# A cross-attention with 16 heads of 16: two passes after one another, or side by side

## The reference

```python
def _L0_xattn_ref(q, k, v, Wq, bq, Wk, bk, Wv, bv, Wo, bo, mask):
    H = 16
    NEG = -10000000000.0
    B, S, D = q.shape
    dk = D // H
    qh = (q @ Wq.T + bq).reshape(B, S, H, dk).transpose(0, 2, 1, 3)
    kh = (k @ Wk.T + bk).reshape(B, S, H, dk).transpose(0, 2, 1, 3)
    vh = (v @ Wv.T + bv).reshape(B, S, H, dk).transpose(0, 2, 1, 3)
    scores = jnp.einsum('bhqd,bhkd->bhqk', qh, kh) / jnp.sqrt(jnp.float32(dk))
    scores = jnp.where(mask[:, None, :, :] == 0, jnp.float32(NEG), scores)
    attn = jax.nn.softmax(scores, axis=-1)
    ctx = jnp.einsum('bhqk,bhkd->bhqd', attn, vh)
    concat = ctx.transpose(0, 2, 1, 3).reshape(B, S, D)
    return concat @ Wo.T + bo
...
    x = x + _L0_xattn_ref(_layernorm(x, axis=-1), ctx_1024, ctx_1024, L0_xattn_Wq, ...
```

## Time and profile before

| | us |
|---|---|
| timed runs | 2060.04, 2058.66, 2054.0 |
| median | 2058.66 |
| profiled execution | 2057.15 |
| its span | 2055.3 |
| mean granted clock of TensorE | 0.878 of full speed |

### The profile page before, as it was taken

How to read it: one execution, slowest core, us unless ns; L and a number is a source line. 1 busy time by engine, 2 the same in 40 slices (tenths; PEclk the granted TensorE clock), 3 DMA queues, 4 the chain that set the end, 5 groups by cost and what they waited for, 6 DMA issues and landing times. The chain is left out here.

```text
span 2055.3 us, 32700 instructions
## 1 busy us (share of the span) xinstructions
PE 1573.8 (77%) x11346; PEld 1345.9 (65%) x11346; DVE 876.4 (43%) x1913; ACT 550.3 (27%) x1311; POOL 336.8 (16%) x401
## 2 busy tenths in 40 slices
PE   2799997539991799999994099999999256691775
PEld 2565664429991688888874099999999244581664
DVE  5443542402224566665665011111111235448896
ACT  1233232102221455454441011111111011231553
POOL 1121120030002333332321400000000511004122
PEclk8999999569996799999995599999999678795787
DMA  4344241158132100000003454224470210101000
GB/s 127 59 76 66 48 69 12 59 200 276 39 113 86 61 7 7 7 7 2 2 1 113 148 195 148 103 67 146 148 270 18 76 47 16 34 26 41 6 15 21
DMA packets 118240, 152.13 MB, mean 74 GB/s; under 512 B 15360, under 2 KB 101376, under 8 KB 118016
## 3 DMA queue, kind: packets, MB, share of 16 engines
q1 hardware_dynamic: 101536, 123.86, 19.6%
q0 software_dynamic: 7680, 18.89, 4.1%
q10 hardware_dynamic: 8928, 8.13, 1.1%
HBM read 113.16 MB, written 24.64 MB: 67 GB/s over the span
## 5 line engine op out<-in xcount | busy, mean ns | idle before, releaser
L1271 PEld LDWEIGHTS f_ph<-f_xgT,f_w 128*128 128x128 f32 x3232 | 373.0, 193 | 21.7 <-issue 18.8
L1271 PE MATMUL f_ph<-f_xgT,f_w 128*128 128x128 f32 x3232 | 374.4, 277 | 16.1 <-DMA f_w<-in_f_w 14.9
L1281 PE MATMUL f_py<-f_w,f_hT 128*128 128x256 f32 x992 | 224.6, 379 | 0.0
L1281 PEld LDWEIGHTS f_py<-f_w,f_hT 128*128 128x128 f32 x992 | 183.7, 190 | 22.6 <-issue 0.2
L1342 DVE TENSOR_TENSOR f_hT<-f_ph,f_gate_o 128x512 f32<-128x512 f32 x78 | 54.0, 692 | 309.3 <-ACT f_gate_o L1305 309.3
L1376 POOL DMA_INDIRECT c_yt<-sorted_y,dest x48 | 45.6, 950 | 649.7 <-issue 648.8
L799 ACT ACTIVATE a_work<-a_ps,a_bias 128x128 f32<-128x128 f32 (+1 forms) x256 | 104.1, 419 | 149.0 <-DVE a_bias L879 91.3
L937 POOL TENSOR_TENSOR a_work<-a_work,a_recip 128x256 f32<-128x256 f32 (+1 forms) x128 | 103.1, 827 | 234.3 <-DVE a_recip L894 234.3
L145 PE MATMUL n_tp<-ident,n_xn 128*128 128x128 f32 x160 | 33.1, 384 | 134.9 <-DVE n_xn L125 134.3
L1305 ACT ACTIVATE f_gate_o<-f_ph 128x512 f32<-128x512 f32 x78 | 46.6, 597 | 295.2 <-PE f_ph L1271 295.1
L145 PEld LDWEIGHTS n_tp<-ident,n_xn 128*128 128x128 f32 x160 | 25.8, 196 | 142.7 <-DVE n_xn L125 135.9
(11 more groups left out here) (307 smaller groups left out, 3103.7 us busy)
## 6 DMA issues: line engine op xcount, KB each, us to landing
f_w<-in_f_w SPq DMA_DIRECT2D x72, 1024.0 KB, 7.2
f_xg<-sorted_x SPq DMA_DIRECT2D x62, 128.0 KB, 2.1
sorted_y<-f_yg ACTq DMA_DIRECT2D x62, 128.0 KB, 1.7
a_qs<-a_part SPq DMA_DIRECT2D x96, 64.0 KB, 5.1
a_ks<-a_part POOLq DMA_DIRECT2D x96, 64.0 KB, 5.3
sorted_x<-zeros SPq DMA_DIRECT2D x1, 4992.0 KB, 16.5
a_ctxT<-in_ctxT SPq DMA_DIRECT2D x16, 256.0 KB, 2.7
sorted_x<-zeros SPq DMA_DIRECT2D x1, 2944.0 KB, 10.2
```

What stands on the lines that cost most here:

```text
L1271: mm = pe.matmul(ph[:, q, n, f * P:(f + 1) * P], w[:, s, k, (q * FQ + f) * P:(q * FQ + f + 1) * P], xgT[:, s, k, :], start=(k == 0), stop= ...
L1281: mm = pe.matmul(py[:, s, 0:D], hT[:, s, f, :], w2[:, s, f, :], start=(f == 0), stop=(f == FT - 1))
```

## The change

- **Order.** The loops are gone; every engine walks the same list of steps k = -16 to 69, written out. At step k stand unit k of the second pass and unit k + 9 (AHEAD) of the first, of all batches counted through. With u = k % 8 and i = k // 8 the other work has its step: projection of the queries, keys, values of batch i + 2 at u = 0, 1, 7; weighing at u = 2, 4, 6, 7, now four heads each; spread_sums of batch i - 1 at 3, its output in two halves at 4 and 5; turn_maxima of batch i + 1 at 6.
- **Banks.** The second pass always has banks 0 and 1 (ST), the first 2 and 3 (SC; the first nine units use both pairs in turn).
- **Parts.** Two float32r parts instead of three bf16 ones, three products (0,0), (0,1), (1,0), 48 rows a head and 50 with minus the maximum in two rows. Two heads of a unit lie in rows 0 to 63 and 64 to 127. Six transfers of 128 KB a batch for queries and for keys. The mask's matmul comes first, the scores are added.
- **Slots.** Three slots of qs, ks, neg, negT, V instead of two; pT holds four heads twice.
- **Queues.** turn_sums and the way back (spread_rows) are issued by ScalarE, at u = 0 and u = 2, behind that step's exponential and ahead of the high part of the queries at u = 0. shift_rows is four transfers instead of three, on SyncE.
- **Start.** Three waits instead of one for the weights; SyncE loads wq, wk and the first inputs, issues the first stack, then loads the rest. GpSimd fills all of ks with ones (128x6144 f32) instead of VectorE's fill of its last 32 rows.

```diff
--- before.py
+++ after.py
...
+    HALF, ROWS = P // 2, 3 * D0
+    AHEAD = U + 1
+    PARTS = ((0, 0, 1), (0, 1, 0))
+    LAND = 16 * len(PARTS[0]) * DK
+    ST, SC, OB, MB = 0, 2, 4, 6
...
-        neg, negT = sb("neg", [P, 2, TB, S], BF16), sb("negT", [P, 2, TB, S], BF16)
-        part = sb("part", [P, 3, 2, DK, S], BF16)
-        rest = sb("rest", [P, 2, DK, S])
-        qs, ks = sb("qs", [P, 2, H, S], BF16), sb("ks", [P, 2, H, S], BF16)
-        V = sb("V", [P, 2, TB, H, W])
-        top_s = sb("top_s", [P, TB, H])
-        mpart, mrest = sb("mpart", [H, 3, S], BF16), sb("mrest", [H, S])
-        pT = sb("pT", [P, 2, 2, TB, S])
+        neg, negT = sb("neg", [P, 3, TB, S], BF16), sb("negT", [P, 3, TB, S], BF16)
+        part = sb("part", [P, 2, 2, DK, S], F32R)
+        qs, ks = sb("qs", [P, 3, U, S], F32R), sb("ks", [P, 3, U, S], F32R)
+        V = sb("V", [P, 3, TB, H, W])
+        top_s = sb("top_s", [P, TB, 2, U])
+        mpart = sb("mpart", [H, 2, S], F32R)
+        pT = sb("pT", [P, 2, G, TB, S])
...
+        def bank(m):
+            return ST if m < AHEAD and m % 2 else SC
+        def to_stack(engine, w, n, b):
 
             for t, which in enumerate(PARTS[w]):
                 if which == n:
-                    for k in range(DK):
-                        engine.dma_start((qs, ks)[w][t * D0:(t + 1) * D0, s, k * HB:(k + 1) * HB, :],
-                                         part[:, n, w, k, :]).then_inc((stacked, k_stacked)[w], 16)
-
-        def every_batch(engine, body):
-
-            with engine.Fori(0, B // 2 - 1) as pair:
-                body(pair * 2, 0, pair, False)
-                body(pair * 2 + 1, 1, pair, False)
-            body(B - 2, 0, B // 2 - 1, False)
-            body(B - 1, 1, B // 2 - 1, True)
+                    for j in range(DK):
+                        engine.dma_start((qs, ks)[w][j * HALF + t * D0:j * HALF + (t + 1) * D0, b % 3, :, :].bitcast(F32),
+                                         part[:, n, w, j, :].bitcast(F32)).then_inc((q_stacked, k_stacked)[w], 16)
+        steps = range(-2 * U, B * U + 6)
...
+            def shut(first, which, b):
+                for j in range(2):
+                    for t in range(TB):
+                        pe.matmul(ps[:, first + j, t * S:(t + 1) * S], consts["identb"][:, :], which[:, b % 3, t, :],
+                                  start=(t == 0), stop=False, skip_group_check=True)
+            def pairs(first, left, right, rows, b, u):
+                for t in range(TB):
                     for j in range(2):
-                        h, bank = 2 * u + j, ps[:, 2 * (u % 2) + j, :]
-                        for t in range(TB):
-                            pe.matmul(bank[:, t * S:(t + 1) * S], qs[0:R, s, h, t * P:(t + 1) * P], ks[0:R, s, h, :],
-                                      start=True, stop=False)
-                            mm = pe.matmul(bank[:, t * S:(t + 1) * S], consts["identb"][:, :], neg[:, s, t, :],
-                                           start=False, stop=True)
-                    mm.then_inc(s_ready, 1)
+                        r = slice(j * HALF, j * HALF + rows)
+                        mm = pe.matmul(ps[:, first + j, t * S:(t + 1) * S], left[r, b % 3, u, t * P:(t + 1) * P],
+                                       right[r, b % 3, u, :], start=False, stop=True, skip_group_check=True)
+                return mm
+            def scores(k):
+                m = k + AHEAD
+                if is_unit(m):
+                    if m % U == 0:
+                        pe.wait_ge(neg_ready, m // U + 1)
+                    if m >= AHEAD:
+                        pe.wait_ge(max_done, m)
+                    elif m >= 2:
+                        pe.wait_ge(max_done, m - 1)
+                    shut(bank(m), neg, m // U)
+                if is_unit(k):
+                    if k >= 1:
+                        pe.wait_ge(exp_done, k)
+                    shut(ST, negT, k // U)
+                if is_unit(m):
+                    if m % U == 0:
+                        pe.wait_ge(q_stacked, (m // U + 1) * LAND)
+                        pe.wait_ge(k_stacked, (m // U + 1) * LAND)
+                    pairs(bank(m), qs, ks, ROWS, m // U, m % U).then_inc(s_ready, 1)
+                if is_unit(k):
+                    if k % U == 0:
+                        pe.wait_ge(mrow_landed, (k // U + 1) * 64)
+                    pairs(ST, ks, qs, ROWS + 2, k // U, k % U).then_inc(st_ready, 1)
...
+            def weigh(b, n):
+                pe.wait_ge(exp_done, b * U + (2 * n + 2))
+                if n == 0:
+                    pe.wait_ge(v_out, b + 1)
+                    pe.wait_ge(mlo_done, b + 1)
+                    if b == 0:
+                        pe.wait_ge(ones_set, 2)
+                if n == NG // 2 and b >= 1:
+                    pe.wait_ge(o_out, 2 * b)
+                for t in range(TB):
+                    for g in range(G):
+                        mm = pe.matmul(O[W * g:W * (g + 1), n, :], V[:, b % 3, t, G * n + g, :],
+                                       pT[:, n % 2, g, t, :], start=(t == 0), stop=(t == TB - 1))
+                mm.then_inc(pv_done, 1)
...
+            for k in steps:
+                i, u = k // U, k % U
+                scores(k)
+                if u == 0 and is_batch(i + 2):
+                    queries(i + 2)
+                if u == 1 and is_batch(i + 2):
+                    keys(i + 2)
+                if u == 3 and is_batch(i - 1):
+                    spread_sums(i - 1)
+                if u in (2, 4, 6) and is_batch(i):
+                    weigh(i, u // 2 - 1)
+                if u in (4, 5) and is_batch(i - 1):
+                    output(i - 1, u - 4)
+                if u == 6 and is_batch(i + 1):
+                    turn_maxima(i + 1)
+                if u == 7 and is_batch(i + 2):
+                    values(i + 2)
+                if u == 7 and is_batch(i):
+                    weigh(i, NG - 1)
...
+            pool.memset(ks[:, :, :, :].bitcast(F32), 1.0).then_inc(set_done, 1)
+            pool.wait_ge(set_done, 1)
+            for b in range(B):
+                stack(b)
...
+            def exps(k):
+                b, u = k // U, k % U
+                act.wait_ge(st_ready, k + 1)
+                if k >= 4:
+                    act.wait_ge(pv_done, k // 2 - 1)
+                act.activation(pT[:, u // 2 % 2, 2 * (u % 2):2 * (u % 2) + 2, :, :].rearrange("p j t n -> p j (t n)"),
+                               ps[:, ST:ST + 2, :], ACT.Exp, scale=float(D0) ** -0.5).then_inc(exp_done, 1)
...
+            def turn_sums(b):
+                act.wait_ge(o_out, b * 2 + 2)
+                for g in range(G):
+                    act.dma_start(sums[g * W:(g + 1) * W, :], oraw[g * W + D0:g * W + D0 + 1, :, :]
+                                 ).then_inc(sums_landed, 16)
+            def spread_rows(b):
+                act.wait_ge(recip_done, b + 1)
+                for g in range(G):
+                    act.dma_start(rrow[g * W + D0:g * W + D0 + 1, :, :], recip[g * W:(g + 1) * W, :]
+                                 ).then_inc(recip_landed, 16)
+            for k in steps:
+                i, u = k // U, k % U
+                if is_unit(k):
+                    exps(k)
+                if u == 0 and is_batch(i - 1):
+                    turn_sums(i - 1)
+                if u == 2 and is_batch(i - 1):
+                    spread_rows(i - 1)
+                if u == 0 and is_batch(i + 2):
+                    high(i + 2, 0, q_proj, q_high)
+                if u == 1 and is_batch(i + 2):
+                    high(i + 2, 1, k_proj, k_high)
...
+            for k in steps:
+                i, u = k // U, k % U
+                if is_unit(k + AHEAD):
+                    maximum(k + AHEAD)
+                if u == 0 and is_batch(i + 2):
+                    low(i + 2, 0, q_high, q_low)
+                if u == 1 and is_batch(i + 2):
+                    low(i + 2, 1, k_high, k_low)
+                if u == 1 and is_batch(i - 1):
+                    reciprocals(i - 1)
+                if u == 2 and is_batch(i + 2):
+                    prepare(i + 2)
+                if u == 3 and is_batch(i - 1):
+                    normalise(i - 1)
+                if u == 4 and is_batch(i):
+                    take_out(i, 0)
+                if u == 5 and is_batch(i - 1):
+                    residual(i - 1)
+                if u == 6 and is_batch(i + 1):
+                    split_maxima(i + 1)
+                if u == 7 and is_batch(i + 2):
+                    add_bias(i + 2)
+                if u == 7 and is_batch(i):
+                    take_out(i, 1)
...
```

More of the change, by code:

```diff
@@ new lines, in queries, with keys @@
+            def queries(b):
+                if b == 0:
+                    pe.wait_ge(qk_in, 16 * 3)
+                if b >= 4:
+                    pe.wait_ge(resid_done, b - 3)
+                project(wq, 0, [xt[:, k, b * S:(b + 1) * S] for k in range(DK)], q_proj)
+            def keys(b):
```

(50 more changed lines are left out.)

375 lines of the change are left out of this document (151 added, 224 removed).

## The result

| | before | after |
|---|---|---|
| median, us | 2056.38 (2050.43 to 2060.04) | 2073.86 (2067.37 to 2079.4) |
| ratio, 95% interval | | 1.0087 [1.0067, 1.0107] |
| profiled execution, its span | 2057.15, 2055.3 | 2070.06, 2068.2 |
| mean granted clock | 0.878 | 0.865 |

The changed kernel is 0.87% slower, where 2020.0 was forecast. Its stretches, columns as in rows 2: the start to the first scores, from there to the scores of step 0, one steady batch, three pieces of the batch behind it (ahead of the spread of the sums, the wait for it, the 10 us from it on), the tail.

The account below looks back on a forecast made before the run. TensorE's own work bounds the 37.4 us steady batch; steps of 29.0 plus waits of 2.6 make 31.6. 74.2 + 26.0 + 158.0 + 29.1 + 25.1 = 312.4 instead of 349.6, gain 37.2: 2020.0 us, range 2005 to 2044.

Parts of the forecast that it names:

- T 74.2: Start: the last first-pass matmul of step 0 comes at 74.2 us.
- landing takes 1.7: Second pass, u = 2: the reciprocals' rows land 1.7 us after issue and are down 3.5 us after that step's exponential.
- the 1.95: TensorE at u = 3 stands about 1.95 us a batch for the reciprocals' rows, range 1.4 to 2.5.
- 5.1 us of landing: Start: the first stack's six issues end at 44, landing takes 5.1 us, so first scores come near 50 instead of 57.6.
- Rival B: Start doesn't move, as stacks share queues with loads or the memset is slow: 8 to 12 us, 2030; chance 0.12.
- rival A: Weighing by V: strips run two at a time, 1.86 instead of 0.99 us, 20 us in all, 2040; chance 0.14.
- the estimate of 1.16: Weighing by V: 16 f32 matmuls in four strips take 1.16 us, 6 us more over the stage.
- The step without extra work: Steady batch: a step with only both passes' scoring, bound by waits for PSUM readers, takes 2.80 us.
- rival C: Changing between full rows, halves and strips empties TensorE: 0.16 us twice a step, 20 in all, 2040; chance 0.05.
- ScalarE's issues: Eight transfers a batch moved to ScalarE's queue, four each at u = 0 and 2: 0.45 us each, ends 0.34 and 0.59.
- Rival D: Granted clock falls to 1.2 GHz because TensorE stands in pieces: 21 us more a batch, 2104 with four; chance 0.05.
- Rival E: No change: the order of waits costs three times as much, 8 us a batch instead of 2.6, 2056; chance 0.05.

Follow-up runs that it names:

- the filled wait: Changed kernel with eleven float32 matmuls ahead of TensorE's wait for the reciprocals' rows, batches 0 to 4: 2066.24 us.
- thin stacks: Kernel with sums and rows going through TensorE, every stacking transfer cut to an eighth of its bytes from batch 0 on: 1998.27 us.
- the start's loads moved: Kernel with sums and rows going through TensorE, loads of ctx 1, wo, sel and second masks waiting for the first stack: 2018.38 us.
- the values' loads first: Kernel with sums and rows through TensorE and values 0 and 1 projected earlier, wv and bv loaded right behind the first masks: 2017.61 us.
- the version without the transfers: Changed kernel with small f32 matmuls turning the sums and spreading the reciprocals instead of transfers: 2019.16 us, ratio to before 0.982.
- the held version: Changed kernel, SyncE and GpSimd issuing stacks from batch 3 on only when the reciprocals' rows of the batch in progress have landed: 2026.84 us.

## Why the prediction was wrong

The forecast for the profiled execution was 50.1 us too low (2020.0, 2070.06). Its terms, by the first exponentials of the batches (84.9, 111.0, 151.9, 193.1, 235.7, 276.8, 317.7, 345.4) and the end of the last weighing (368.6):

| term | forecast | measured | off |
|---|---|---|---|
| first exponential of batch 0 (T 74.2 + 0.5) | 74.7 | 84.9 | +10.2 |
| batch 0 | 26.0 | 26.1 | +0.1 |
| batches 1 to 5 | 158.0 | 206.7 | +48.7 |
| batch 6 | 29.1 | 27.7 | -1.4 |
| batch 7 | 25.1 | 23.2 | -1.9 |
| tail, to the end of x | 20.2 | 17.2 | -3.0 |
| all behind the stage (1685.5 before) | 1685.5 | 1682.4 | -3.1 |

The offs add up to 49.6; the 0.5 that is missing is the one put to T, from which the forecast counted its batch 7.

- **The step that failed: "landing takes 1.7".** The wait itself was in the sum, with its place and its queue. Its size came from a row measured where nothing else is in flight, and was carried to a place inside the stack's traffic. In the five batches the waits were 10.2, 10.0, 10.5, 8.9 and 8.8 us, 9.7 in the mean, for the 1.95: +7.7 a batch. The low clock with it is +1.8 to 2.3 (the filled wait); together 9.5 to 10.0, where the batch was 9.7 over. For a quiet place the 1.95 was even too dear: with the stack held the wait was 0.8 to 0.9. The range of 1.4 to 2.5 varied only the issues' price. It could have been seen: 0.42 of 37.4 us is 15.7 us of all 16 engines for each batch, and "SyncE and GpSimd issue 6 transfers each, due seven steps later: nothing" asked only whether the stack would be late, not what would stand beside it. The list of steps has the keys' parts at u = 1 and the rows at u = 2.
- **The start.** The first matmul came at 32.26 (34), the parts earlier than forecast, the memset took 5.22 and was hidden. But 5.1 us of landing is again one transfer's median, not the whole stack's: 10.8 us after the last issue, GpSimd's (42.7), first scores at 53.55 (50). And the path forgot that the first scores of batch 1 stand at step -1, ahead of step 0: they waited until 78.75 for the second stack, and 3.78 of values at the low clock came behind. With thin stacks the first exponential starts at 72.2. So it is mostly the stacks' bytes; the loads beside them are worth 0.7 to 1.9 us (the start's loads moved, the values' loads first). Rival B had this mechanism ("the stacks share the queues") with the lesser sharer; its 2030 was for the start alone, and its place in the steady batch was not in it.
- **What TensorE does: right.** Sixteen strip matmuls take 1.07 (0.99); rival A fell, and the estimate of 1.16 by the Trainium skill's page TensorE: Matmul & The Clock Gate (Measured speedup vs the span model) is as near from the other side. The step without extra work takes 3.0 (2.80). In the version without the transfers 30.5 us hold 1.84 of turning, so 29.0 for the rest was no underestimate. If a change of tiling mode cost rival C's 0.16 us twice a step, a batch would be 2.6 us over that; so C fell too.
- **ScalarE's issues.** 2.47 for four, 0.62 each: over the upper end of 0.59, and worth 0.7 us at each of the two places at most (4 x 0.17).
- **The clock.** Rival D's mechanism did act, mainly through the wait of 10 us, and for some 2 us a batch instead of 21. Pieces of 2 us can do it too: the held version has 0.64 over 4.8 us in a batch whose longest wait is 1.6. In the version without the transfers it is 1.00. Rival E's form (waits cost three times) came nearest: the batch stands 12.3 over the steps' sum of 29.0, not 8, and nearly all of it at one wait.

## What to carry to other kernels

A landing time belongs to the traffic beside it: before a small transfer is moved, list what every queue has in flight at its new place, and take the DMA engines' share times the stretch as an estimate of how long a burst of those bytes will be under way (here 15.7 us, where 16.4 to 17.2 passed). A row from a quiet moment is the lower end of the range, the burst's own length the upper one. If a small transfer must cross a burst, send it first (one wait on each queue was worth 2.3% here: 2026.84 against 2073.86), or do it without a transfer: 1.84 us of TensorE replaced 8.8 to 10.5 of standing. In a start, count to the last landing of the whole burst, and look which scores stand ahead of the first useful one.

## What was not expected of the hardware

- A 4 KB transfer took 1.8 us alone and 10.8 from its last issue beside the stack, though it had ScalarE's queue for itself. The packets' turns explain part; why a wait of 5.8 us stays beside packets of 1 KB, in step with the stack's own landings, isn't settled.
- GpSimd's queue carries the stack in 4 KB packets, SyncE's in packets of 1 KB; transfers of the same size landed in 8.1 and 4.5 us (medians).
- The stack's bytes go slowly: with the queries' stack under way the DMA engines move 158 GB/s at a share of 0.98 (198 to 201 us of the changed kernel), with loads alone 338 GB/s at 1.07 (213 to 214 us). A transfer of the stack writes 16 partitions, a load 128; whether that is the reason was not tried, and a stack in fewer, wider transfers stays untested.
- The granted clock was 0.63 in the stretch of the wait and 0.70 in the 10 us behind it, then 1.00; it was at 0.5 from 206.0 to 219.7 us, where the wait is 203.4 to 213.8. In the held version it fell to 0.64 over 4.8 us in a batch whose longest wait was 1.6 us.
- A change between full rows, half rows and 32-column strips, twice a step, cost nothing that shows: 30.33 us busy in 30.50, and 28.7 for the work that the step-by-step sum without it put at 29.0. (Busy time alone wouldn't tell, since a record includes its latency.)
